# Reordering TensorE between the threshold verdict and the first output projections, and a projection that waits for a residual instead of a variance

## The chip, the cores and the metric

The kernel runs on one core of one Trainium2 chip. The metric is the device time of one execution in microseconds (us). A core has five engines that run instruction streams of their own and meet at semaphores: TensorE (PE; its weight loads are PEld), VectorE (DVE), ScalarE (ACT), GpSimd (POOL) and SyncE (SP), which issues most of the DMAs.

## The reference, cut to what matters

Sixteen sequences of 128 rows with 256 features, x, pass through four gated layers, each added to x. The two in the middle matter here.

```python
# layer 2: a sparse feed-forward net, on h = layernorm(x), 2048 rows
z = h @ ternary_quant(W_syn).T + b_syn            # 2048 x 1024
thresh = top_k(z, 102)[0][:, -1:]                 # a threshold for every row
hidden = where(z >= thresh, relu(z), 0.0)
out = hidden @ ternary_quant(W_out).T + b_out     # the output projection
x = x + tanh(g_ffn[0]) * (layernorm(h + out) * gamma + beta)

# layer 3: a long convolution; k = v = ctx, q = layernorm(x)
kv = einsum('bhil,bhjl->bijhl', k_, v_)
y = irfft(rfft(kv) * rfft(ssm_kernel)) + kv * D   # does not depend on x
x = x + tanh(g_xattn[1]) * einsum('bijhl,bhil->bjhl', y, q_)
```

Layer 1 is an attention over features, layer 4 a mixture of 64 experts with six chosen for every row.

## The kernel before, in words

The rows are worked on in 16 tiles (b = 0 to 15) of 128 rows. The kernel has stages: attention and z for all tiles; the search for the 16 x 128 thresholds; the batch pipeline (projection, second norm, layer 3's last product, routing), in which tiles go in pairs through a loop v_ = 0 to 7 (NPAIR = 8) that every engine's program writes out in an order of its own; then the experts, and the sum of their outputs. No planner orders anything: each engine executes its list in order, and semaphore waits stand in it.

**The convolution of layer 3** needs no x. It is made head by head, 16 of them, k = 0 to 15: `conv(k)` (TensorE, L932) does six products of 344 columns on the products of k and v (`kv_in`, by DMA), a Toeplitz matrix, and a diagonal (`tdiag_ready`). `keep_conv(k)` (ScalarE, L1311) copies four PSUM banks out and counts `co_ready`. SyncE stores the copy to `co_rows` in HBM (L513, `co_out`). AHEAD = 14 of them, k = 0 to 13, stand beside the threshold search, in two sets of PSUM banks in turn: 0 to 3 for even k, 4 to 7 for odd k. Numbers 14 and 15 use banks 4 to 7 and stand among the first projections. When all sixteen stores have landed, SyncE loads `co_rows` back by pairs of tiles, `load_group(g)` (L517, the DMA at L520), and then issues 36 fills of `xs_rows` (L443) before group 2.

**The verdict.** VectorE finds a threshold for each row in a few steps and tells whether any row failed: `verdict` (L1823) makes `bad` and counts `bad_ready`. TensorE sums `bad` over partitions with one narrow matmul into the first column of bank 0 (L960). VectorE copies the sum as an integer (L1849), makes the hidden tiles 0 and 1 by the thresholds (L1846, counting `hid_made`), loads the integer, skips the repair branch when it is zero, and counts `hid_ready` by two (L1886).

**A tile's projection.** `turn_hidden(b)` (TensorE, L962) transposes hidden tile b with eight transposes into banks 1 and 2; it waits until tile b-1 was copied out. `evac_hidden(b)` (ScalarE, L1351) copies it to SBUF. `project(b)` (TensorE, L972) is 16 matmuls of 256 columns into bank 0. VectorE's `second_block(b)` (L1922) makes hidden tile b+2, then adds the projection to the residual `H2` (`residual`, L1895), takes row sums, aggregates, and writes mean and variance (L1920, counting `var3_ready`); between these stand the four steps of tile b-1, which end in `x` after layer 2 and its own variance. GpSimd raises the variances to -0.5.

**Then layer 3's last product**: `query3` (ScalarE, L1358), `turn_q` (TensorE), `evac_q` (ScalarE), and `times_q(h)` (VectorE, L1946; its first instruction is L1959), which waits for the group of `co_rows` that was loaded back (`kv_in`) and for its query. The first, `times_q(0)`, stands on VectorE behind `second_block(2)`; `second_block(3)` stands behind it. A pair's scatters to the experts' rows (`scatters`, GpSimd, L781) wait for the routing of that pair, and the first pair's also for all the fills.

The orders around the change, before:

```python
# TensorE
for k in range(AHEAD): conv(k)
pe.wait_ge(co_ready, AHEAD); pe.wait_ge(bad_ready, 1)      # L958, L959
pe.matmul(psum[:, 0, 0:1], onesf, bad).then_inc(ones_done)  # L960
conv(AHEAD); turn_hidden(0); turn_hidden(1); project(0); conv(AHEAD + 1)
# then, for v_ = 0: turn_hidden(2), project(1), turn_hidden(3), project(2)
# ScalarE
keep_conv(AHEAD); evac_hidden(0); evac_hidden(1); keep_conv(AHEAD + 1)
# then, for v_ = 0: evac_hidden(2), evac_hidden(3)
```

Of the kernel before, what the change touches and what calls it, by code (L numbers as in the profile page):

```python
# [18 lines left out]
def build(nc, x, ctxn, ctxT, ctxH, toep, gates_in, wsynT, woutT, bsyn, bout, gamma, beta, ssm_D,  # L19
          gateT, wexp, wd1, wsgu, wsd, out):  # L20
    f32, bf16, i32, u32 = mybir.dt.float32, mybir.dt.bfloat16, mybir.dt.int32, mybir.dt.uint32
    ALU = mybir.AluOpType
# [4 lines left out]
    NT = 16  # L27
    D = 256
# [34 lines left out]
    AHEAD = 14  # L63
# [21 lines left out]
    with ExitStack() as ctx:  # L85
# [12 lines left out]
        H2 = sb("H2", [P, NT, D])  # L98
# [29 lines left out]
        stats = sb("stats", [P, NT + 2, 6])  # L128
# [10 lines left out]
        wsc = sb("wsc", [P, 2])  # L139
# [119 lines left out]
        psum = ctx.enter_context(nc.psum_tensor("psum", [P, 8, 512], f32))  # L259
# [25 lines left out]
        var3_ready, rstd3_ready = sem("var3_ready"), sem("rstd3_ready")  # L285
# [25 lines left out]
        hid_made = sem("hid_made")  # L311
# [12 lines left out]
        conv_done, co_ready = sem("conv_done"), sem("co_ready")  # L324
# [70 lines left out]
        def alone(eng, name):  # L395

            eng.sem_inc(tick[name], 1)
# [469 lines left out]
        def _(pe):  # L867
# [64 lines left out]
            def conv(k):  # L932
                w = 8 * NCOL
                first = 4 * (k % 2) if k < AHEAD else 4
                pe.wait_ge(tdiag_ready, 2 * k + 2)
                if k < DIRECT:
                    src = kv_sq[:, head_of(k) % 2].rearrange("p m b r -> p (m b r)")
                    pe.wait_ge(kv_ready, head_of(k) + 1)
                else:
                    src = kvs[k % 4]  # L940
                    pe.wait_ge(kv_in[k % 4], 16 * ((k - DIRECT) // 4) + 16)
                if k >= 2:
                    pe.wait_ge(co_ready, k - 1 if k < AHEAD else k)
                for g in range(2):
                    r = [src[:, (16 * m_ + 8 * g) * NCOL:(16 * m_ + 8 * g + 8) * NCOL] for m_ in range(2)]
                    pe.matmul(psum[:, first + g, 0:w], tdiags[k % 4], r[0], start=True, stop=True)  # L946
                    pe.matmul(psum[:, first + 2 + g, 0:w], toeps[k % 4][:, 1, :], r[0], start=True, stop=False)  # L947
                    m = pe.matmul(psum[:, first + 2 + g, 0:w], tdiags[k % 4], r[1], start=False, stop=True)  # L948
                m.then_inc(conv_done, 1)
# [3 lines left out]
            pe.wait_ge(hT_ready, NT)  # L953
            pe.wait_ge(w_ready, 2)
            pe.wait_ge(z_ready, NT)
            for k in range(AHEAD):
                conv(k)
            pe.wait_ge(co_ready, AHEAD)  # L958
            pe.wait_ge(bad_ready, 1)  # L959
            pe.matmul(psum[:, 0, 0:1], onesf[:, :], bad[:, :], start=True, stop=True).then_inc(ones_done, 1)  # L960

            def turn_hidden(b):  # L962
                par = b % 2
# [8 lines left out]
            def project(b):  # L972
                par = b % 2
                pe.wait_ge(hidT_ready, b + 1)
                if b:
                    pe.wait_ge(var3_ready, b)
                for c in range(8):
                    m = pe.matmul(psum[:, 0, 0:D], hidT[:, par, c * P:(c + 1) * P], wout[:, c, :],  # L978
                                  start=(c == 0), stop=(c == 7))
                m.then_inc(o_done, 1)  # L980
# [78 lines left out]
                                      wsd_sb[0:fw, c, :], start=(c == 0), stop=(c == 2))  # L1059
                m.then_inc(sy_done, 1)  # L1060

            conv(AHEAD)
            turn_hidden(0)
            turn_hidden(1)
            project(0)
            conv(AHEAD + 1)
            for v_ in range(NPAIR):
                c, u, w = v_ - 1, v_ - 2, v_ - 3
                if u >= 0:
                    x3_turn(u)  # L1070
                if c >= 0:
                    turn_q(2 * c)
                if 2 * v_ + 2 < NT:
                    turn_hidden(2 * v_ + 2)
                project(2 * v_ + 1)
                if w >= 0:
                    shared_up(w, 2)
                if c >= 0:
                    turn_q(2 * c + 1)
                if w >= 0:  # L1080
                    shared_down(w)
                if u >= 0:
                    if u == 0:
                        pe.wait_ge(co_ready, NH)
                        pe.wait_ge(ws_in, 64)
                    r_turns(u)
                if 2 * v_ + 3 < NT:
                    turn_hidden(2 * v_ + 3)
                if u >= 0:
                    logits(u)  # L1090
                if 2 * v_ + 2 < NT:
                    project(2 * v_ + 2)
                if 0 <= u < NPAIR - 3:
                    ranks(u)
                    shared_up(u, 0)
                    shared_up(u, 1)

            a, b = NPAIR - 2, NPAIR - 1
# [142 lines left out]
        def _(act):  # L1241
# [69 lines left out]
            def keep_conv(k):  # L1311
                par = k % 2
                first = 4 * par if k < AHEAD else 4
                act.wait_ge(conv_done, k + 1)
                if co_turn[k]:
                    act.wait_ge(co_out[co_slot[k]], 16 * co_turn[k])
                for l in range(2):
                    m = act.activation(co[co_slot[k]].rearrange("p (g a l n) -> p l g a n", g=2, a=4, l=2)[:, l],
                                       psum[:, first + 2 * l:first + 2 * l + 2, 0:8 * NCOL].rearrange("p g (a n) -> p g a n", a=4),
                                       ACT.Copy)  # L1320
                m.then_inc(co_ready, 1)
# [29 lines left out]
            def evac_hidden(b):  # L1351
                act.wait_ge(hidT_full, b + 1)
                if b >= 2:
                    act.wait_ge(o_done, b - 1)
                act.activation(hidT[:, b % 2, :].rearrange("p (a n) -> p a n", a=2), psum[:, 1:3, :],  # L1355
                               ACT.Copy).then_inc(hidT_ready, 1)
# [55 lines left out]
                act.wait_ge(sy_done, w + 1)  # L1412
                act.activation(base[:, w], s_y[:, :], ACT.Identity, scale=tg[:, 3:4]).then_inc(base_ready, 1)

            keep_conv(AHEAD)
            evac_hidden(0)
            evac_hidden(1)
            keep_conv(AHEAD + 1)
            for v_ in range(NPAIR):
                c, u, w = v_ - 1, v_ - 2, v_ - 3  # L1420
                if c >= 0:
                    query3(2 * c)
                if u >= 0:
                    keep_rows(u)
                if c >= 0:
                    evac_q(2 * c)
                if 2 * v_ + 2 < NT:
                    evac_hidden(2 * v_ + 2)
                if w >= 0:
                    shared_silu(w, 2)  # L1430
                if c >= 0:
                    query3(2 * c + 1)
                    evac_q(2 * c + 1)
                if u >= 0:
                    normalise(u)
                if w >= 0:
                    shared_out(w)
                if u >= 0:
                    evac_x(u)
                if 2 * v_ + 3 < NT:  # L1440
                    evac_hidden(2 * v_ + 3)
                if 0 <= u < NPAIR - 3:
                    keep_logits(u)
                    exponents(u)
                    shared_silu(u, 0)
                    shared_silu(u, 1)
# [66 lines left out]
        def _(dve):  # L1513
            v = {"at": 0, "k": 0}

            def mark(ins):

                v["k"] += 1
                ins.then_inc(v_step, 1)
                return v["at"] + v["k"]  # L1520
# [374 lines left out]
            def residual(b, par):  # L1895
                dve.wait_ge(o_done, b + 1)
                dve.wait_ge(h2b_done, b + 1)
                return mark(dve.scalar_tensor_tensor(H2[:, b, :], psum[:, 0, 0:D], wsc[:, 1:2], H2[:, b, :], ALU.mult, ALU.add))

            def centre(b):  # L1900
                dve.wait_ge(rstd3_ready, b + 1)
# [6 lines left out]
            def row_sums(src, slot_, made):  # L1908
                dve.wait_ge(v_step, made)
                alone(dve, "dve")  # L1910
                return mark(dve.bn_stats(stats[:, slot_, :], src))
# [10 lines left out]
            def second_block(b, between=None):  # L1922
                tile, behind = b < NT, b >= 1
                if b + 2 < NT:
                    make_hidden(b + 2, b % 2)
                if tile:
                    at_h = residual(b, b % 2)
                if behind:
                    at_x = centre(b - 1)
                if between is not None:  # L1930
                    mean_shift(between)
                if tile:
                    at_h = row_sums(H2[:, b, :], NT, at_h)
                if behind:
                    at_x = add2(b - 1, at_x)
                if tile:
                    at_h = aggregate(NT, at_h)
                if behind:
                    at_x = row_sums(X[:, b - 1, :], NT + 1, at_x)
                if tile:  # L1940
                    variance(b, NT, at_h, var3_ready)
                if behind:
                    at_x = aggregate(NT + 1, at_x)
                    variance(b - 1, NT + 1, at_x, var4_ready)
# [332 lines left out]
```

## Time and profile before

| what | value |
|---|---|
| median of three runs | 716.46 us (712.61 to 722.75) |
| the profiled execution | 720.17 us, of which its span is 718.4 us |
| mean granted TensorE clock of the span | 0.944 of full speed |
| TensorE matmul busy | 611.0 us (85% of the span) |
| VectorE busy | 471.6 us (66%) |
| GpSimd busy | 451.8 us (63%) |
| ScalarE busy | 296.9 us (41%) |

The span runs from the first to the last instruction of the profiled execution; times in the trace count from its start. Busy times are sums over stages with different limits, so a stage is read from its own stretch. The threshold search ends near 180 us, the batch pipeline lies between 180 and 415 us, the experts' matmuls between 423 and 651 us.

### The profile page before, as it was taken

How to read it: one execution, taken by the hardware profiler on the slowest of the kernel's cores; microseconds unless marked ns; L12 is line 12 of the kernel's file. 1: busy time of each engine (PE TensorE's matmuls, PEld its weight loads, DVE VectorE, ACT ScalarE, POOL GpSimd, SP SyncE). 2: the span in 40 equal slices, each digit the busy share in tenths (PEclk: the TensorE clock that was granted, in tenths of full speed). 3: DMA queues.
4: the chain of work that ended last, by engine and by line, in shares of the span. 5: the costliest groups of instructions: out<-in, count | busy, mean ns of one | idle time of the engine just before them, and what ended most of it. 6: DMA issues, size and time to landing. Idle time of an engine off the chain costs nothing.

```text
span 718.4 us, 11813 instructions
## 1 busy us (share of the span) xinstructions
PE 611.0 (85%) x3072; PEld 470.5 (65%) x3072; DVE 471.6 (66%) x1596; ACT 296.9 (41%) x657; POOL 451.8 (63%) x512
## 2 busy tenths in 40 slices
PE   4789998769788798989857879999999999999920
PEld 2455554446566677877746668888888888878710
DVE  5898987999259988898895534444454454544515
ACT  3157777958233454555455223322233232323200
POOL 2697845782022287878787724777777777786560
PEclk9799999989899999999989899999999999999965
DMA  7579715869959943953333768999999999996878
GB/s 243 181 255 317 258 46 186 231 181 304 317 195 376 373 160 130 309 203 115 150 109 129 237 217 209 240 284 256 281 249 284 258 263 278 264 271 105 231 122 295
DMA packets 97822, 163.69 MB, mean 228 GB/s; under 512 B 10848, under 2 KB 65568, under 8 KB 96736
## 3 DMA queue, kind: packets, MB, share of 16 engines
q1 hardware_dynamic: 76864, 135.16, 56.9%
q0 software_dynamic: 20608, 27.82, 20.2%
q8 instruction: 23, 0.38, 0.2%
q14 instruction: 39, 0.32, 0.1%
q10 hardware_dynamic: 288, 0.01, 0.0%
HBM read 91.24 MB, written 71.71 MB: 227 GB/s over the span
## 4 chain that ended last, share of the span: by engine, by line
PE 57%; DVE 14%; issue 11%; POOL 9%; DMA 6%; ACT 1%; SPq 1%; DVEq 0%; POOLq 0%; ACTq 0%
PE psum L1164 12%; PE psum L1177 7%; PE psum L1168 6%; PE psum L904 5%; POOL xs_rows L781 5%; PE psum L1182 4%; PE psum L1148 4%; PE psum L1048 3%; PE psum L978 3%; PE psum L946 3%; PE psum L947 3%; PE psum L948 2%; DMA acc<-hh,toki 2%; POOL acc L847 2%; DVE Z L1962 1%
## 5 line engine op out<-in xcount | busy, mean ns | idle before, releaser
L847 POOL DMA_INDIRECT acc<-hh,toki x128 | 187.9, 1468 | 80.4 <-DVE hh L2173 40.9
L2173 DVE TENSOR_SCALAR hh<-psum,wtok 96x256 f32<-96x256 f32 (+3 forms) x128 | 55.8, 478 | 131.8 <-issue 110.7
L781 POOL DMA_INDIRECT xs_rows<-Z,slot x96 | 101.6, 1058 | 33.5 <-issue 23.4
L1481 ACT ACTIVATE qT<-psum 128x384 f32<-128x384 f32 (+3 forms) x64 | 33.5, 524 | 91.9 <-PE psum L1148 91.0
L694 POOL TENSOR_TENSOR rstd<-mv,neghalf 128x1 f32<-128x1 f32 x48 | 32.4, 685 | 59.9 <-DVE mv L1920 41.5
L978 PE MATMUL psum<-wt,hh 128*128 128x256 f32 x256 | 59.2, 385 | 4.5 <-DVE mv L1920 3.4
L904 PE MATMUL psum<-wt,hTs 128*128 128x512 f32 x128 | 59.7, 609 | 0.6 <-ACT hTs L1260 0.6
L978 PEld LDWEIGHTS psum<-wt,hh 128*128 128x128 f32 x256 | 48.0, 192 | 11.3 <-ACT hh L1355 4.6
L1164 PE MATMUL psum<-qT,kve 128*128 128x192 f32 (+3 forms) x256 | 52.8, 350 | 0.0
L1048 PE MATMUL psum<-Z,wt 128*128 128x256 f32 (+1 forms) x192 | 48.7, 406 | 0.8 <-DVE H L2035 0.8
L1487 ACT ACTIVATE H<-psum 128x192 f32<-128x192 f32 (+3 forms) x64 | 22.2, 348 | 63.7 <-PE psum L1164 62.0
L1164 PEld LDWEIGHTS psum<-qT,kve 128*128 128x128 f32 x256 | 43.6, 194 | 1.5
L1164 PE MATMUL psum<-qT,Z 128*128 128x192 f32 (+3 forms) x224 | 44.2, 340 | 0.0
L1048 PEld LDWEIGHTS psum<-Z,wt 128*128 128x128 f32 (+1 forms) x192 | 36.4, 194 | 7.8 <-DVE H L2035 1.0
L904 PEld LDWEIGHTS psum<-wt,hTs 128*128 128x128 f32 x128 | 23.5, 194 | 24.0 <-issue 24.0
L1148 PE MATMUL psum<-ident,Z 96*128 96x96 f32 (+3 forms) x256 | 35.9, 263 | 2.2 <-DMA Z<-xs_rows 2.2
L1164 PEld LDWEIGHTS psum<-qT,Z 128*128 128x128 f32 x224 | 37.0, 190 | 0.6
L1148 PEld LDWEIGHTS psum<-ident,Z 96*128 96x128 f32 (+3 forms) x256 | 27.4, 142 | 15.0 <-issue 12.2
L1274 ACT ACTIVATE hh<-Z,thr 128x1024 bf16<-128x1024 f32 x32 | 36.7, 1146 | 1.2 <-DVE Z L1655 0.6
L1182 PE MATMUL psum<-wt,hh 48*96 48x256 f32 (+3 forms) x240 | 33.4, 397 | 0.0
L1489 ACT ACTIVATE H<-psum 48x192 f32<-48x192 f32 (+3 forms) x64 | 21.8, 341 | 23.5 <-PE psum L1168 23.5
L876 PE MATMUL psum<-hh,kve 128*128 128x256 f32 x64 | 20.3, 447 | 12.2 <-DVE hh L1601 7.7
(368 smaller groups left out, 1434.9 us busy)
## 6 DMA issues: line engine op xcount, KB each, us to landing
xs_rows<-fill SPq DMA_DIRECT2D x64, 272.0 KB, 4.5
kve<-in_wexp SPq DMA_DIRECT2D x32, 496.0 KB, 4.1
Z<-in_wexp SPq DMA_DIRECT2D x30, 496.0 KB, 4.3
kve<-co_rows SPq DMA_DIRECT2D x8, 1376.0 KB, 7.5
kv_rows<-Z SPq DMA_DIRECT2D x8, 688.0 KB, 3.9
kve<-kv_rows SPq DMA_DIRECT2D x8, 688.0 KB, 7.9
Z<-xs_rows SPq DMA_DIRECT2D x24, 204.0 KB, 4.2
Z<-xs_rows SPq DMA_DIRECT2D x16, 272.0 KB, 3.1
```

What stands on the lines that cost most here:

```text
L781: pool.indirect_dma_start(out=xs_rows[:, :], out_offset=bass.IndirectOffsetOnAxis(ap=slot[:, t, k:k + 1], axis=0), in_=H[:, t, :], in_offs ...
L847: pool.indirect_dma_start(out=acc[a][:, :], out_offset=bass.IndirectOffsetOnAxis(ap=toki[0:p, g, j:j + 1], axis=0), in_=y_sb[0:p, s, j, :] ...
L904: m = pe.matmul(psum[:, 4 + 2 * par + c, :], hTs[:, par, k, :], wsyn[:, k, c * 512:(c + 1) * 512], start=(k == 0), stop=(k == 1))
L978: m = pe.matmul(psum[:, 0, 0:D], hidT[:, par, c * P:(c + 1) * P], wout[:, c, :], start=(c == 0), stop=(c == 7))
L1048: m = pe.matmul(s_up[w][c][0:fw, g * CAP:(g + 1) * CAP], wsgu_sb[:, k, g * FSH + f0:g * FSH + f0 + fw], xTs[:, w, k, :], start=(k == 0), s ...
L1148: m = pe.transpose(pT[par][:, (2 * k + j) * p:(2 * k + j + 1) * p], xs_sb[0:p, s, j, k * P:(k + 1) * P], ident[0:p, 0:p])
L1164: m = pe.matmul(pA[par][:, g * CAP:g * CAP + 2 * p], w[:, k, g * P:(g + 1) * P], xT[:, par, k, 0:2 * p], start=(k == 0), stop=(k == 1))
L1168: m = pe.matmul(pC[par][0:GU - 2 * P, 0:2 * p], w[:, k, 2 * P:GU], xT[:, par, k, 0:2 * p], start=(k == 0), stop=(k == 1))
L1177: pe.matmul(pY[q][0:p, j * D:(j + 1) * D], hid0[:, q, j * p:(j + 1) * p], lastd0[:, s - 4 + q, :] if last else wd0_sb[s + q], start=(j == ...
L1182: m = pe.matmul(pY[q][0:p, j * D:(j + 1) * D], hid1[r, q, j * p:(j + 1) * p], lastd1[r, (s - 4) // 2, :] if last else wd1_sb[r, s + q, :], ...
L1274: act.activation(ajunk[:, i % 4, :], z[:, t, :], ACT.Sign, bias=points[:, t:t + 1], scale=-1.0, accum_out=total[:, t:t + 1]).then_inc(cnt_ ...
L2173: m = dve.tensor_scalar(y_sb[0:p, s, j, :], pY[par][0:p, j * D:(j + 1) * D], wtok[0:p, g, j:j + 1], None, ALU.mult)
```

## The change

On TensorE the verdict's sum is put between the convolutions of heads 12 and 13, and waits for 13 copies, not 14. Head 13 follows it. Heads 14 and 15 each move one place back: 14 from before the first transposes to behind `project(0)`, 15 from behind `project(0)` to behind `project(1)`. ScalarE's copies of 14 and 15 move to match. Besides, `project(b)` no longer waits for the variance of tile b-1 (`var3_ready`) but for the residual that reads bank 0 (`hid_made`, now counted on by `residual`), and the row sums of the residual wait on that same count.

```diff
@@ TensorE
-            for k in range(AHEAD):
+            for k in range(AHEAD - 1):
                 conv(k)
-            pe.wait_ge(co_ready, AHEAD)
+            pe.wait_ge(co_ready, AHEAD - 1)
             pe.wait_ge(bad_ready, 1)
             pe.matmul(psum[:, 0, 0:1], onesf[:, :], bad[:, :], start=True, stop=True).then_inc(ones_done, 1)
+            conv(AHEAD - 1)
...
             def project(b):
                 pe.wait_ge(hidT_ready, b + 1)
                 if b:
-                    pe.wait_ge(var3_ready, b)
+                    pe.wait_ge(hid_made, b + 2)
...
-            conv(AHEAD)
             turn_hidden(0)
             turn_hidden(1)
             project(0)
-            conv(AHEAD + 1)
+            conv(AHEAD)
...
                 project(2 * v_ + 1)
+                if v_ == 0:
+                    conv(AHEAD + 1)
@@ ScalarE
-            keep_conv(AHEAD)
             evac_hidden(0)
             evac_hidden(1)
-            keep_conv(AHEAD + 1)
+            keep_conv(AHEAD)
...
                 if 2 * v_ + 2 < NT:
                     evac_hidden(2 * v_ + 2)
+                if v_ == 0:
+                    keep_conv(AHEAD + 1)
@@ VectorE
             def residual(b, par):
-                return mark(dve.scalar_tensor_tensor(H2[:, b, :], psum[:, 0, 0:D], wsc[:, 1:2], H2[:, b, :], ALU.mult, ALU.add))
+                dve.scalar_tensor_tensor(H2[:, b, :], psum[:, 0, 0:D], wsc[:, 1:2], H2[:, b, :], ALU.mult, ALU.add).then_inc(hid_made, 1)
...
                 if tile:
-                    at_h = residual(b, b % 2)
+                    residual(b, b % 2)
...
                 if tile:
-                    at_h = row_sums(H2[:, b, :], NT, at_h)
+                    dve.wait_ge(hid_made, b + 3)
+                    alone(dve, "dve")
+                    at_h = mark(dve.bn_stats(stats[:, NT, :], H2[:, b, :]))
```

## Rows read from the trace of the kernel before

**Rows 1.** The page's busy time, share of the span and instructions.

```profile
PE 611.0 (85%) x3072; PEld 470.5 (65%) x3072; DVE 471.6 (66%) x1596; ACT 296.9 (41%) x657; POOL 451.8 (63%) x512
```

**Rows 2.** The chain that ended last, 181 to 246: start us, us, what.

```profile
181.26 1.39 ACT co L1318 x2
...
182.69 0.38 PE psum L960 x2
183.07 1.68 issue
184.75 1.49 PE psum L946 x2
...
191.24 1.38 ACT qT L1318 x2
...
208.41 3.71 PE psum L978 x16
...
214.76 0.43 DVE Z L1959
...
217.70 1.11 issue
...
245.68 0.24 DVE mask L2005
```

**Rows 3.** The timeline from 177 to 186, VectorE and ScalarE.

```profile
177.79 1.38 ACT L1318 ACTIVATE wt<-psum 128x688 f32<-128x688 f32 x2 [0.65 <-PE psum L948]
...
178.11 0.15 DVE L1828 TENSOR_SCALAR bad<-bad 128x1 f32<-128x1 f32 x1
...
183.18 0.16 DVE L1849 CAST bad_i<-psum 128x1 int32<-128x1 f32 x1 [3.81 <-PE psum L960]
183.25 2.47 DVE L1846 SCALAR_TENSOR_TENSOR hh<-Z,thr 128x1024 f32<-128x1024 f32 x2
```

**Rows 4.** The timeline from 194 to 208, TensorE, ScalarE and SyncE.

```profile
194.57 3.62 PE L978 MATMUL psum<-wt,hh 128*128 128x256 f32 x16
...
198.03 0.74 PE L946 MATMUL psum<-kve,hs 128*128 128x344 f32 x2
...
201.50 1.04 PE L968 MATMUL psum<-ident,hh 128*128 128x128 f32 x8
201.70 1.38 ACT L1318 ACTIVATE qT<-psum 128x688 f32<-128x688 f32 x2 [5.90 <-PE psum L948]
...
202.37 3.62 PE L978 MATMUL psum<-wt,hh 128*128 128x256 f32 x16
...
203.11 0.36 SPq L513 DMA_DIRECT2D co_rows<-qT  x1
...
207.34 0.81 SPq L520 DMA_DIRECT2D kve<-co_rows  x2
```

**Rows 5.** DMA issues at 174.1, 203.1, 207.3 and 241.5 to 242.5: us to landing.

```profile
kve<-kv_rows SPq DMA_DIRECT2D x1, 688.0 KB, 10.5
...
co_rows<-qT SPq DMA_DIRECT2D x1, 688.0 KB, 4.2
...
kve<-co_rows SPq DMA_DIRECT2D x1, 1376.0 KB, 5.7
...
xs_rows<-fill SPq DMA_DIRECT2D x2, 272.0 KB, 3.9
```

**Rows 6.** By stretch: length, busy PE, PEld, DVE, ACT, POOL, PE clock, DMA, GB/s.

```profile
181.00:184.70 3.70, 0.60 (x3) 0.30 (x2) 1.52 (x3) 1.38 (x2) 1.02 (x2) 0.83 1.13 296
184.70:190.20 5.50, 5.45 (x10) 3.36 (x11) 1.02 (x1) 0.00 (x0) 0.45 (x1) 0.50 1.06 374
190.20:195.00 4.80, 3.20 (x22) 2.60 (x21) 1.28 (x1) 2.52 (x4) 0.00 (x0) 0.99 1.18 282
```

**Rows 7.** TensorE's waits from 205 to 235: us in total, times, longest us.

```profile
PE psum L978 <- DVE mv L1920: 3.4, 3, 1.5
```

**Rows 8.** The timeline at the first scatter, GpSimd.

```profile
248.47 2.00 POOL L781 DMA_INDIRECT xs_rows<-Z,slot  x1 [7.02 <-DVE slot L2028]
```

## The prediction

> **What bounds the kernel now.** I read the page's busy shares first, and only to see that they decide nothing: TensorE has 85% and VectorE 66% of the span [rows 1], averages over stages. The question is what holds up the stretch that the change touches, so I went on to the chain that ended last between 181 and 246 us [rows 2]. The reader should see three parts in it. First the verdict: the chain goes through ScalarE's copy of head 13 (181.26), the narrow sum (182.69), a pause of 1.68 us, and head 14 on TensorE from 184.75. Then the projections, with head 15 between them, up to the third one at 208.41. Then it passes to VectorE: the first `times_q` begins at 214.76 and the chain stays on VectorE to the routing mask at 245.68. So for the end it counts when that first `times_q` starts, not when a projection does.
>
> Then the timeline around the verdict [rows 3]: `bad` is made at 178.11 + 0.15 = 178.26, but its integer is read at 183.18 only. In between TensorE finished head 13 and ScalarE copied it, because the sum waits for 14 copies. Last the rows of the other thing that `times_q(0)` needs, the convolutions loaded back [rows 4, 5]: the store of head 15 is issued at 203.11 and takes 4.2 us to land; the load of group 0 goes out at 207.34, and lands 5.7 us later, at 213.04. That is only 214.76 - 213.04 = 1.72 us before `times_q(0)` began. This second chain runs through head 15, which the change moves behind one more projection.
>
> **The change part by part.** The pitches come from rows 4. Head 15's first matmul comes at 198.03 and the transposes behind it at 201.50: a head costs 3.47 us of TensorE. From its first matmul to its copy's start: 201.70 - 198.03 = 3.67. To the issue of its store: 203.11 - 198.03 = 5.08. Transposes to projection: 202.37 - 201.50 = 0.87. A projection to what follows it: 198.03 - 194.57 = 3.46. From a copy of a head to the first projection, with two transposed tiles and ScalarE's copies between: 194.57 - 191.24 = 3.33 [rows 2, 4].
>
> (1) The sum. It now waits for `bad` (178.26) and the copy of head 12, which ends at 177.79 + 1.38 = 179.17 [rows 3]; before it began 0.05 after the copy, so at 179.2 instead of 182.69, 3.5 us earlier. Queued behind it on TensorE is head 13, which before ran without a pause; this adds an idle TensorE from head 12's end (177.8) to 179.2, and head 13 begins behind the sum's 0.38, at 179.59. VectorE's tiles 0 and 1 move with the sum: from 183.25 + 2.47 = 185.72 to 182.2. The thresholds still count one branch after that; before, head 14 covered it, now head 13 does, which ends near 183.2.
>
> (2) Heads 13 to 15 and the first projections. Copy of 13 starts at 179.59 + 3.67 = 183.26. `project(0)` starts 3.33 later, 186.59, against 194.57: 8.0 earlier. Of these, 2.8 are the half clock of head 14 (184.75 to its copy at 191.24 is 6.49, against 3.67), 1.7 the pause in front of it, the rest the sum's place. That pause I read as the load of head 14's products, issued at 174.1 with 10.5 to land, so 184.6 [rows 5]. In the new order head 14 starts at 186.59 + 3.46 = 190.05, and the load is hidden with 5.4 us to spare. Transposes of tile 2 at 193.52, `project(1)` at 194.39, head 15 at 197.85. Before it was 198.03. So the 8.0 us are spent on what now stands in front of head 15 besides, a head, a tile's transposes and a projection, 3.47 + 0.87 + 3.46 = 7.8, and head 15 moves by -0.2.
>
> (3) After head 15: transposes at 201.32, `project(2)` at 202.19 against 208.41, 6.2 earlier. VectorE would reach `times_q(0)` at 214.76 - 6.2 = 208.5.
>
> (4) What is late next. The store of head 15 goes out at 197.85 + 5.08 = 202.93, group 0 is issued 0.18 earlier than before and lands at 212.86. `times_q(0)` starts there, near 212.9, not at 208.5. SyncE's queue holds nothing else against it: the stores of 12 to 14 are issued earlier or land before 207. The gain at the handover is 214.76 - 212.9 = 1.86, rounded 1.8; the other 4.4 us are idle time of VectorE. Bounds: nothing at all, if the load lands 1.7 later, and 6.3, if it does not bind.
>
> (5) The projection's wait for the variance. TensorE waited for it three times, 3.4 us in all and at most 1.5 [rows 7], and all three lie between 205 and 235 us. The first is already in step (3), where `project(2)` is held by the transposes alone. The other two lie where the chain is on VectorE, so they pay nothing at the end; without them TensorE idles elsewhere. Cost below: none, since the new count rises at an earlier instruction of the same block. On VectorE the row sums wait for the same instruction as before by another semaphore; no instruction is added.
>
> (6) Downstream. Through 245.68 VectorE's list is the chain; it moves by 1.8. The first scatter at 248.47 waited for a slot [rows 8] and would be due at 246.7; the last fills, issued by 242.5 with 3.9 to land, are in by 246.4 [rows 5]. That is close, but holds. After it everything follows the same orders, so I carry 1.8 to the end: 718.4 for the profiled execution (720.17). That one lies 3.7 above the median of the runs shown; measured times are medians, so I forecast 716.46 - 1.8 = 714.7 us.
>
> **The rivals.** (A) The clock falls, and head 15 comes late: slower. In 181.00 to 184.70 TensorE was busy 0.60 us, and the next 5.5 us were granted 0.50, the lower level of 1.2 GHz [rows 6]. The new order has a pause of 1.4 us before the sum, and between head 13 and `project(0)` 3.3 us with nothing but 16 transposes. At the lower level a head takes 6.49 instead of 3.67, 1.77 times as long; a projection would take 6.1 instead of 3.46, the transposes nearly 1 more, so head 15 comes about 3.4 later, group 0 at 216.3, and `times_q(0)` 1.5 late: 718.0 us. It decides from the point where head 15 is more than 1.9 later than I put it. Against it: in 190.20 to 195.00 the same transposes, with the same pause for ScalarE between them, were granted 0.99 [rows 6]. For it: the pause before the sum comes on top.
>
> The Trainium skill, in "TensorE: Matmul & The Clock Gate", section "Part 4: PE-mode transpose", says that transposes do not count as activity for the full clock as matmuls do. By that rule the stretch before `project(0)` looks idle to the chip and rival A is what happens, 718.0 instead of 714.7. The row of 190.20 to 195.00, with 0.99, speaks against it here.
>
> (B) The gain is given back: 716.5. VectorE's new wait before `times_q(0)` leaves TensorE without work between `project(3)` and tile 5's transposes, some 6 us, after which it could run at the lower level until the first pair's transposes of layer 3 are late by 1 to 2 us; or the last fills hold the first scatter. That would also be the case in which the edits do what they say, and none of it is on the path.
>
> (C) Group 0 does not bind, and all of step (3) stays: 716.46 - 6.3 = 710.2. It needs head 15's store and reload to end by 208.5, and the rows give them 4.2 and 5.7 from 202.9 on; and the fills would then stop the first scatter after some 2 us.
>
> **How the numbers follow.** Forecast 0.60, A 0.17, B 0.18, C 0.05. All four lie between 710.2 and 718.0. The runs before spread from 3.9 below to 6.3 above their median, which is more than the cases differ, so the range is 708.5 to 720.5: the cases with about 2 us of spread at each end. Two per cent is 14.3 us, about what a measurement of this kernel can tell from no change, and no case reaches it. Only an error in which the whole trace is misread would: faster 0.03, within 0.95, slower 0.02.
>
> **What would show it.** Right: the integer of `bad` is read near 179.7 and the first hidden tiles are ready by 182.3; `project(0)` near 186.6 and `project(2)` near 202.2; VectorE idle for some 4 us before L1959, which starts within 0.2 us of group 0's landing near 212.9; no wait of L978 on L1920; the first scatter near 246.7. Wrong: a granted clock of 0.5 between 180 and 195, head 15 after 199, or an L1959 that starts well before 212, or a first scatter that has not moved though L1959 has.

## The result, and the profile after

The change makes no difference of two per cent, but it is slower, not faster as forecast. Its median is 722.29 us over 20 runs, that of the kernel before 718.48 over 20 runs that include the three shown; the ratio is 1.0071, 95% interval 1.0048 to 1.0095, some 5.1 us. (The ratio is an estimate over the runs and not the quotient of the two medians, which differ by 3.8 us.) The forecast was 1.8 us less, 714.7, and the measured median lies above the upper end of the range, 720.5. Of the 7.6 us between 714.7 and 722.29, 2.0 are the base that the forecast started from: the three runs shown had a median of 716.46, the twenty have 718.48. The profiled execution took 720.8 us with a mean granted clock of 0.942, much like that of before. On the page nothing moves that could tell why:

```profile
PE 610.8 (85%) x3072; PEld 472.8 (66%) x3072; DVE 470.7 (65%) x1596; ACT 296.3 (41%) x657; POOL 451.3 (63%) x512
```

Against [rows 1] the busy times differ by 1 us or less, except for the weight loads, which overlap. So the stretch has to be read. The timeline of the changed kernel, 181 to 251 us (start, us, engine, line; in brackets the idle time in front and what ended it):

```profile
181.07 0.15 DVE L1831 TENSOR_SCALAR bad<-bad 128x1 f32<-128x1 f32 x1
...
181.37 0.35 PE L960 MATMUL psum<-bad,onesf 128*128 128x1 f32 x2 [3.65 <-DVE bad L1831]
...
181.58 1.03 PE L946 MATMUL psum<-kve,tdiag 128*128 128x344 f32 x2
...
187.03 1.38 ACT L1320 ACTIVATE co<-psum 128x688 f32<-128x688 f32 x2 [7.89 <-PE psum L948]
...
205.97 3.62 PE L979 MATMUL psum<-wt,hh 128*128 128x256 f32 x16
...
216.82 0.43 DVE L1964 TENSOR_TENSOR Z<-kve,hTs 128x256 f32<-128x256 f32 x1 [4.51 <-DMA kve<-co_rows]
...
250.53 2.00 POOL L781 DMA_INDIRECT xs_rows<-Z,slot  x1 [7.02 <-DVE slot L2033]
```

The reader should see four things. The verdict came at 181.07, not at 178.11 [rows 3] (two executions, of which more below), and since head 13 now stands behind the sum, TensorE waited 3.65 us for it. The third projection (205.97) did come earlier, by 2.4 us against 208.41 [rows 2]. The store of head 15 (206.70, in the next view) came 3.6 later than 203.11 [rows 4]. And the first `times_q` stood idle for 4.51 us until the load of group 0 had landed, and began at 216.82 instead of 214.76, 2.06 late; the first scatter at 250.53 is 2.06 behind [rows 8]. The chain of waits says the same; where [rows 2] had the third projection it now has two transfers (start us, us, what):

```profile
206.70 4.27 DMA co_rows<-qT
...
211.04 5.75 DMA kve<-co_rows
```

TensorE's waits between 205 and 235 us hold no wait of a projection on the variance any more, against three in [rows 7]; the one large wait left is that of tile 5's transposes on VectorE:

```profile
PE psum L969 <- DVE hh L1849: 7.4, 1, 7.4
```

It ends at 222.19, and behind it the grant fell to 0.50 in the last of the windows below. The first scatter did not feel it: it stands 33.71 us behind the first `times_q` here, as it did before (248.47 - 214.76).

The windows of the changed kernel, with busy times by engine and, behind them, the granted TensorE clock as a share of full speed:

```profile
177.70:181.40 3.70, 0.05 (x2) 0.06 (x1) 3.49 (x11) 1.38 (x2) 0.00 (x0) 1.00 1.09 326
181.60:185.50 3.90, 3.90 (x10) 2.39 (x10) 3.21 (x6) 0.00 (x0) 1.03 (x2) 0.56 1.14 296
185.50:190.00 4.50, 2.90 (x18) 2.15 (x18) 1.28 (x1) 2.29 (x3) 0.46 (x1) 1.00 1.07 378
...
220.00:225.00 5.00, 2.81 (x11) 2.63 (x12) 4.82 (x12) 0.80 (x1) 0.53 (x2) 0.50 0.99 338
```

After the idle 3.70 us head 13 ran near the lower level, 0.56. In the stretch of the 16 transposes that rival A feared (185.50 to 190.00) the grant was 1.00.

### The profile page after: what moved, and what is told of

Its sections match the earlier page's. It is cut to its first block, busy times and chain, and to the rows that moved or that the text cites. A ratio compares the mean times of both kernels' runs of the same rounds, so it can differ in the third digit from the quotient of the medians.

```text
span 719.0 us, 11813 instructions
## 1 busy us (share of the span) xinstructions
PE 610.8 (85%) x3072; PEld 472.8 (66%) x3072; DVE 470.7 (65%) x1596; ACT 296.3 (41%) x657; POOL 451.3 (63%) x512
## 4 chain that ended last, share of the span: by engine, by line
PE 52%; DVE 17%; issue 12%; DMA 8%; POOL 7%; ACT 3%; SPq 0%; DVEq 0%; POOLq 0%; ACTq 0%
PE psum L1166 12%; PE psum L1179 7%; PE psum L1170 6%; PE psum L904 5%; POOL xs_rows L781 5%; PE psum L1184 4%; PE psum L1150 4%; PE psum L1049 3%; PE psum L979 3%; DVE hh L1815 3%; DMA acc<-hh,toki 2%; POOL acc L847 2%; PE psum L876 2%; DVE Z L1966 1%; DVE Z L1967 1%
```

## The experiments

Four theories were put to the chip. H: the end follows the store of head 15, through its reload, and the change puts more in front of that store. S: the sum's place does it, by the pause and the half clock behind it. W: the new wait for the residual does it. P: the projections decide. A fifth, L, came up on the way and stands with its run. Ratios are against the kernel before, run beside it, each over 12 runs of the kernel, with the 95% interval. Where a head moves on TensorE, ScalarE's copy of it moves to match (in the sixth experiment its order already fits); those lines are left out of the diffs.

**Only the new wait** (before, with the second half of the change; VectorE's lines, as in the change, are left out):

```diff
-                    pe.wait_ge(var3_ready, b)
+                    pe.wait_ge(hid_made, b + 2)
```

> The kernel before with one part of the change: a projection waits for the last tile's residual instead of its variance; TensorE's and ScalarE's orders stay. Theory H (the change is slower because head 15's store, and with it the reload of group 0, comes later): no difference, ratio 0.998 to 1.002, the store of head 15 near 203 us. Theory S (the sum of the verdict in front of head 13 makes TensorE pause and then run at half clock, that alone costs the time): no difference either. Theory W (the new wait does the harm, by letting projections run where they disturb VectorE or the transposes): slower, ratio near 1.007.

Measured: 719.13 us, ratio 1.0008 (0.9976 to 1.0040). W falls. The timeline of this kernel showed something unforeseen; the store was expected near 203:

```profile
182.41 0.38 PE L960 MATMUL psum<-bad,onesf 128*128 128x1 f32 x2 [1.47 <-ACT co L1318]
...
198.28 0.36 SPq L513 DMA_DIRECT2D co_rows<-qT  x1
...
208.51 0.46 DVE L1961 TENSOR_TENSOR Z<-kve,hTs 128x256 f32<-128x256 f32 x1 [0.24 <-DMA kve<-co_rows]
```

The sum (182.41) is close to where it was in [rows 2] (182.69), and the order from there to head 15 is that of before; yet the store is out 15.87 us behind the sum, not 20.42.

**Only the order** (the change, with the old wait back):

```diff
-                    pe.wait_ge(hid_made, b + 2)
+                    pe.wait_ge(var3_ready, b)
```

> The changed kernel with the variance wait put back in the projection: the order alone. H and S: as slow as the whole change, ratio 1.005 to 1.009, store of head 15 near 206 to 207 us. W: no slower than before, ratio 1.000.

Measured: 722.92 us, ratio 1.0060 (1.0028 to 1.0092). The order alone is as slow as the whole change. Its timeline, and its windows before and in head 13:

```profile
181.57 0.35 PE L960 MATMUL psum<-bad,onesf 128*128 128x1 f32 x2 [3.08 <-DVE bad L1831]
...
205.21 0.36 SPq L513 DMA_DIRECT2D co_rows<-qT  x1
...
215.66 0.43 DVE L1964 TENSOR_TENSOR Z<-kve,hTs 128x256 f32<-128x256 f32 x1 [4.83 <-DMA kve<-co_rows]
```

```profile
178.40:181.50 3.10, 0.10 (x1) 0.00 (x0) 2.89 (x11) 1.38 (x2) 0.00 (x0) 1.00 1.07 358
181.60:185.50 3.90, 3.90 (x15) 2.46 (x16) 3.55 (x7) 0.00 (x0) 1.03 (x2) 1.00 1.14 310
```

Head 13 was granted 1.00 here, and still the store is 23.64 us behind the sum. No clock is needed for the loss.

**The sum back behind head 13**, the heads 14 and 15 where the change has them:

```diff
-            for k in range(AHEAD - 1):
+            for k in range(AHEAD):
                 conv(k)
             pe.wait_ge(co_ready, AHEAD - 1)
...
-            conv(AHEAD - 1)
```

> The changed kernel with the sum of the verdict put back behind head 13 (it still waits for 13 copies only); heads 14 and 15 stay one place back. S: the loss is gone, ratio 0.998 to 1.002, because TensorE no longer pauses in front of head 13. H: a loss remains, ratio 1.002 to 1.008: by the rows of before the sum at 181.3, first projection at 187.4, head 15 at 198.7 and its store at 203.7, against 203.1, and 2 to 3 us later than that if the clock falls in the pause before the transposes.

Measured: 724.05 us, ratio 1.0080 (1.0047 to 1.0114). The pause in front of the sum is gone and the loss is not. A pause and a half clock came behind the sum instead, so this run alone does not clear the clock; the run before it, with the loss at full clock, does. Together they let S fall. Timeline and windows:

```profile
182.81 0.28 PE L960 MATMUL psum<-bad,onesf 128*128 128x1 f32 x2
...
208.57 0.36 SPq L513 DMA_DIRECT2D co_rows<-qT  x1
...
218.63 0.43 DVE L1963 TENSOR_TENSOR Z<-kve,hTs 128x256 f32<-128x256 f32 x1 [4.44 <-DMA kve<-co_rows]
```

```profile
183.20:187.30 4.10, 1.05 (x8) 0.86 (x8) 2.86 (x5) 1.19 (x2) 0.75 (x2) 1.00 1.14 300
187.40:194.20 6.80, 5.66 (x18) 4.88 (x19) 1.26 (x1) 2.02 (x2) 0.45 (x1) 0.50 1.09 341
```

With no head behind the sum TensorE was busy 1.05 us of 4.10, and the next 6.80 us were granted 0.50. This is the fall that rival A described, in a neighbour of the change. Idle time and transposes stand together in that stretch, so it cannot be told which of them brought it.

**The heads back, the sum early** (the change, with 14 and 15 in their old places):

```diff
+            conv(AHEAD)
             turn_hidden(0)
             turn_hidden(1)
             project(0)
-            conv(AHEAD)
+            conv(AHEAD + 1)
...
-                if v_ == 0:
-                    conv(AHEAD + 1)
```

> The changed kernel with heads 14 and 15 back in their old places (14 in front of the first transposes, 15 behind the first projection); the sum stays in front of head 13. S: as slow as the change, ratio 1.005 to 1.009. H: not slower than before, ratio 0.995 to 1.001, head 15's store issued at 200.2 to 202.5 us, the first product of layer 3 on VectorE 0.6 to 2.9 us earlier than the 214.76 of before.

Measured: 719.84 us, ratio 1.0009 (0.9981 to 1.0038). The loss goes with the heads' places, so H holds. In the profiled execution the store was later than the 200.2 to 202.5 that H expected, and `times_q(0)` no earlier than in [rows 2], but 0.28 later; timeline, and the window of head 13:

```profile
182.05 0.35 PE L960 MATMUL psum<-bad,onesf 128*128 128x1 f32 x2 [3.30 <-DVE bad L1829]
...
204.85 0.36 SPq L513 DMA_DIRECT2D co_rows<-qT  x1
...
215.04 0.43 DVE L1962 TENSOR_TENSOR Z<-kve,hTs 128x256 f32<-128x256 f32 x1 [0.21 <-DMA kve<-co_rows]
```

```profile
182.20:187.40 5.20, 5.20 (x14) 3.12 (x14) 3.42 (x6) 0.00 (x0) 1.13 (x2) 0.67 1.10 329
```

The verdict was late again, TensorE waited 3.30 us for it, and head 13 was granted 0.67. The early sum had bought a pause.

**Only head 15 moved back** (before, nothing else):

```diff
             project(0)
-            conv(AHEAD + 1)
...
                 project(2 * v_ + 1)
+                if v_ == 0:
+                    conv(AHEAD + 1)
```

> The kernel before with one edit: head 15 behind the second projection instead of the first (TensorE and ScalarE). Theory H (the end follows the store of head 15 by its reload): one tile's transposes and a projection more in front of it, 0.87 + 3.46 = 4.3 us, so its store 4.3 us after where the same execution would have had it, near 202.6 to 207.4, and slower by 2.6 to 4.3 us (the smaller where the reload has slack), ratio 1.0035 to 1.006. A rival, theory P (the end follows the projections; head 15 does not matter): no slower, since the projections come 3.5 us earlier, ratio at most 1.000.

Measured: 722.53 us, ratio 1.0059 (1.0030 to 1.0087).

```profile
184.92 0.38 PE L960 MATMUL psum<-bad,onesf 128*128 128x1 f32 x2 [1.47 <-DMA kve<-kv_rows]
...
206.27 0.36 SPq L513 DMA_DIRECT2D co_rows<-qT  x1
...
216.69 0.43 DVE L1961 TENSOR_TENSOR Z<-kve,hTs 128x256 f32<-128x256 f32 x1 [4.80 <-DMA kve<-co_rows]
```

One move costs what the whole change costs. `times_q(0)` is 31.77 us behind the sum and was idle for 4.80 in front of it: the projections were ready, so P falls and H holds.

**Head 15 in front of the first projection** (before, the other way):

```diff
             turn_hidden(1)
+            conv(AHEAD + 1)
             project(0)
-            conv(AHEAD + 1)
```

> The kernel before with one edit: head 15 in front of the first projection, behind the two tiles' transposes. H: its store 3.5 us earlier, near 194.8 to 199.6; the reload then does not bind, the first product of layer 3 follows the third projection instead, which keeps its place, so a gain of 0 to 1.7 us, ratio 0.997 to 1.000. P: slower by up to 3.5 us for the first projection's later start, ratio up to 1.005.

Measured: 718.43 us, ratio 1.0009 (0.9978 to 1.0040).

```profile
180.72 0.38 PE L960 MATMUL psum<-bad,onesf 128*128 128x1 f32 x2 [1.47 <-ACT co L1318]
...
193.14 0.36 SPq L513 DMA_DIRECT2D co_rows<-qT  x1
...
209.39 0.43 DVE L1959 TENSOR_TENSOR Z<-kve,hTs 128x256 f32<-128x256 f32 x1
```

The store is out 12.42 us behind the sum, group 0 lands at 205.02, and `times_q(0)` does not wait for it: it stands 6.34 us behind the third projection (203.05). The reload now has 4.4 us to spare, and that buys nothing, since the projections are next; the third stands 22.33 us behind the sum, against 21.17 in the second profile of before, below.

**Four fills moved** from SyncE's loop over the heads to the first stage. The loop also issues the heads' loads; two of the four fills stand in front of head 14's load, two behind it. Theory L: the pause and the half clock behind the sum, 4.5 us, come from that load being behind the fills.

```diff
-                    if DIRECT // 2 <= k < AHEAD - 2:
+                    if DIRECT // 2 <= k < DIRECT:
...
+                if 10 <= b < 14:
+                    fill_rows(b + 16, b + 17)
```

> The kernel before with four fills of xs_rows (heads 8 to 11 of SyncE's store loop) moved into the first stage. Theory L (in some executions of before head 14 waits for its products' load, issued behind fills, and runs at half clock after the pause): the load of head 14 issued near 171 and landed before 182, no pause between the verdict's sum and head 14, head 15's store near 198 as in the execution of the first experiment, time 1 to 5 us shorter, ratio 0.993 to 0.999. If the loads behind fills do not matter: 1.000.

Measured: 717.64 us, ratio 1.0002 (0.9972 to 1.0033). A miss for L: the pause is gone from its profile, and by the ratio the time has not followed (the medians differ by 1.8 us, 717.64 against 719.46).

```profile
182.49 0.38 PE L962 MATMUL psum<-bad,onesf 128*128 128x1 f32 x2 [1.47 <-ACT co L1320]
...
182.73 0.82 PE L948 MATMUL psum<-kve,hs 128*128 128x344 f32 x2
...
198.36 0.36 SPq L515 DMA_DIRECT2D co_rows<-qT  x1
...
210.01 0.42 DVE L1961 TENSOR_TENSOR Z<-kve,hTs 128x256 f32<-128x256 f32 x1
```

Head 14 follows the sum in 0.24 us, and the store comes 15.87 us behind the sum, to the hundredth as in the run of the wait alone, where the fills stood in their place. That raised the question whether before's pause was ever typical.

**Before and the change, profiled once more.**

> The kernel before once more, for a second profile of it. H and L: if its span is some 4 us shorter than the first profile's 718.4, the store of head 15 lies near 198 to 199 and no half clock follows the verdict's sum; if it is as long, the store lies near 203. The verdict is expected near 180.5 to 182.4, as in the five other profiles, not at 178.3.

> The changed kernel once more, for a second profile. H: the first product of layer 3 starts within 0.1 us of group 0's landing, its store of head 15 23.6 to 25.3 us behind the verdict's sum, against 15.9 in the kernel before where nothing pauses; the sum waits for the verdict, which is 2 to 4 us behind the end of head 12.

Measured: 719.11 and 723.35 us, one run each. The second profile of before, timeline and the window of head 14 and the transposes:

```profile
184.96 0.38 PE L960 MATMUL psum<-bad,onesf 128*128 128x1 f32 x2 [1.47 <-ACT co L1318]
...
185.20 0.82 PE L946 MATMUL psum<-kve,hs 128*128 128x344 f32 x2
...
200.83 0.36 SPq L513 DMA_DIRECT2D co_rows<-qT  x1
...
206.13 3.69 PE L978 MATMUL psum<-wt,hh 128*128 128x256 f32 x16 [1.54 <-DVE mv L1920]
...
212.48 0.43 DVE L1959 TENSOR_TENSOR Z<-kve,hTs 128x256 f32<-128x256 f32 x1
```

```profile
185.20:192.00 6.80, 5.20 (x28) 3.75 (x28) 3.83 (x4) 2.29 (x3) 0.46 (x1) 1.00 1.09 348
```

No pause, clock 1.00, and again 15.87 from the sum to the store and 27.52 to `times_q(0)`, where the first profile had 20.42 and 32.07 [rows 2 to 4]. Neither case of the expectation came: the span, 717.4, is only 1.0 shorter than the first, and yet there is no half clock, and the store is at 200.83. Of the 4.55 us saved behind the sum, 2.27 were lost in front of it (184.96 against 182.69) and 1.2 behind `times_q(0)`. So one execution's time does not tell whether it had the pause. The second profile of the change:

```profile
182.00 0.38 PE L960 MATMUL psum<-bad,onesf 128*128 128x1 f32 x2 [1.47 <-ACT wt L1320]
...
205.67 0.36 SPq L513 DMA_DIRECT2D co_rows<-qT  x1
...
215.96 0.43 DVE L1964 TENSOR_TENSOR Z<-kve,hTs 128x256 f32<-128x256 f32 x1 [4.67 <-DMA kve<-co_rows]
```

```profile
182.00:190.00 8.00, 6.40 (x34) 4.87 (x35) 4.03 (x4) 2.75 (x4) 2.11 (x3) 1.00 1.09 345
190.00:200.00 10.00, 10.00 (x48) 8.09 (x47) 2.45 (x5) 2.86 (x4) 1.88 (x2) 1.00 0.99 276
```

Here the sum waits 1.47 us for ScalarE's copy, as the prediction had it and not for the verdict, as had been expected by then, and the clock is 1.00 throughout. The store is 23.67 us behind the sum, and 23.67 - 15.87 = 7.8, the very figure of step (2).

**The change with head 15 directly behind head 14**, in front of tile 2's transposes and `project(1)`:

```diff
             conv(AHEAD)
+            conv(AHEAD + 1)
...
-                if v_ == 0:
-                    conv(AHEAD + 1)
```

> The changed kernel with head 15 directly behind head 14, in front of tile 2's transposes and the second projection; all else as changed. Theory H: the store of head 15 comes 4.3 us earlier for the work that it passes, less some 1.6 us in which it waits for the copy of head 14 out of the same banks, so 2.7 us earlier than in the changed kernel (22.3 us or less behind the verdict's sum, instead of 23.6 to 25.3), and about half of the loss is gone, ratio to before 1.002 to 1.005. If the place of head 15 did not matter: 1.006 to 1.008 as the change.

Measured: 720.08 us, ratio 1.0016 (0.9991 to 1.0040); the value lies a little under the 1.002 to 1.005 that H expected, the interval overlaps that range and holds 1 as well, and it leaves out the 1.006 to 1.008 of a place that does not matter. In the profile the store is 21.13 us behind the sum, and the reload still comes last:

```profile
180.23 0.38 PE L960 MATMUL psum<-bad,onesf 128*128 128x1 f32 x2 [1.47 <-ACT wt L1319]
...
201.36 0.36 SPq L513 DMA_DIRECT2D co_rows<-qT  x1
...
211.59 0.46 DVE L1962 TENSOR_TENSOR Z<-kve,hTs 128x256 f32<-128x256 f32 x1 [0.24 <-DMA kve<-co_rows]
```

**What the experiments point to**: before's order, head 15 in front of `project(0)`, the new wait, and the four fills moved (the edits of the first, the sixth and the seventh experiment together).

> A try at a version faster than both: the kernel before with the projection waiting for the residual (first experiment), head 15 in front of the first projection, and four fills moved into the first stage. H: the reload has slack (store of head 15 some 12.4 us behind the sum), the third projection starts 19.3 us behind the sum instead of 21.2, and the first product of layer 3 follows it by 6.3: 25.7 us behind the sum instead of 27.5 in the kernel before, a gain of about 1.8 us, ratio 0.996 to 1.000. If neither the reload nor the third projection decides: 1.000.

Measured: 716.75 us, ratio 0.9966 (0.9934 to 0.9997), some 2.4 us faster than before, with an interval that only just leaves out 1; against before, the change has 1.0071, so it is faster than the change, too.

```profile
187.51 0.38 PE L962 MATMUL psum<-bad,onesf 128*128 128x1 f32 x2 [1.47 <-ACT co L1320]
...
213.40 0.43 DVE L1963 TENSOR_TENSOR Z<-kve,hTs 128x256 f32<-128x256 f32 x1
```

`times_q(0)` is 25.89 us behind the sum, 1.6 less than in the second profile of before, and it follows the third projection again (207.00), which now starts right behind its transposes, without the 1.54 us for the variance.

**All profiles side by side.** In each of the 13 the last instruction ends 498.1 to 501.8 us behind the start of `times_q(0)`, with no order between the kernels (498.1 and 501.6 in the two profiles of the change), so what an edit changes is when that starts. The spread of 3.7 us is close to the size of the effects, though: a single profile shows the mechanism and not the time. Where the reload comes last it starts 0.02 to 0.03 us behind group 0's landing; elsewhere 6.3 to 6.4 us behind the third projection. From the store to the landing are 9.9 to 10.4 us (11.9 in the sixth experiment, whose store alone took 6.2). All columns are us; "sum ahead of old place" is how much earlier the sum is than 8.57 us behind the first matmul of head 12, where before's order has it (182.69 - 174.12). The last column but one is the distance to `times_q(0)` less 27.52, less the column before it.

| kernel | sum to store of 15 | sum to `times_q(0)` | comes last | sum ahead of old place | so against before | measured |
|---|---|---|---|---|---|---|
| before, first profile | 20.42 | 32.07 | projection | 0 | +4.6 | |
| before, second | 15.87 | 27.52 | projection | -0.1 | +0.1 | |
| change, first profile | 25.33 | 35.45 | reload | 1.3 | +6.6 | +5.1 (3.4 to 6.8) |
| change, second | 23.67 | 33.96 | reload | 3.5 | +3.0 | the same |
| order only | 23.64 | 34.09 | reload | 1.8 | +4.8 | +4.3 (2.0 to 6.6) |
| sum behind 13 | 25.76 | 35.82 | reload | 1.3 | +7.0 | +5.7 (3.4 to 8.2) |
| heads in place | 22.80 | 32.99 | reload | 1.6 | +3.9 | +0.6 (-1.4 to 2.7) |
| 15 behind 14 | 21.13 | 31.36 | reload | 3.5 | +0.4 | +1.1 (-0.6 to 2.9) |
| 15 back | 21.35 | 31.77 | reload | -0.6 | +4.9 | +4.2 (2.2 to 6.3) |
| wait only | 15.87 | 26.10 | reload | -0.1 | -1.3 | +0.6 (-1.7 to 2.9) |
| 15 first | 12.42 | 28.67 | projection | 0 | +1.2 | +0.6 (-1.6 to 2.9) |
| fills early | 15.87 | 27.52 | projection | 0 | 0 | +0.1 (-2.0 to 2.4) |
| all together | 12.41 | 25.89 | projection | 0 | -1.6 | -2.4 (-4.7 to -0.2) |

The measured column is the ratio less one, times 718.48. By the difference of the medians each entry would be 0.2 to 1.9 us lower. Of the profiles beside a measured value all but two lie inside its interval. The second of the change is just under it (3.0 against 3.4). "Heads in place" lies above it, 3.9 against at most 2.7. The low clock of its head 13 does not explain that: the execution profiled took 719.73 us, and the median of its twelve runs is 719.84. Why these runs lose less than the profile's distances say is open. The wait alone has the other sign, inside its interval.

## Why the prediction was wrong

- **Step (1), the sum 3.5 us earlier: overestimated.** It was measured at 3.5 in one profile of the change, and at 1.3 in the other. The step put the verdict where [rows 3] had it, 4.1 us behind the first matmul of head 12. Over the 13 profiles it comes 3.2 to 7.1 us behind that (181.22 - 174.09 = 7.1 in the change). In before's order head 13 covers this, since the sum stands behind it anyway; in the change TensorE stands idle for it, 3.65 us at most, and may run head 13 at a lower granted clock: its first matmul to its copy was 5.45 us, not 3.67. Why VectorE's verdict moves so much from one execution to another was not found.
- **Step (2), head 15 moved by -0.2: this is the step that failed.** It spent a gain of 8.0 us (3.5 sum, 2.8 half clock, 1.7 pause) on 7.8 of extra work. The 7.8 is right: 23.67 - 15.87. So is the distance that follows from the step: 202.93 - 179.2 = 23.7 from the sum to the store, 23.67 in the second profile of the change. What was wrong is what it was compared with. But the 2.8 and the 1.7 belonged to the one profiled execution of before; its second profile, the wait alone and the moved fills have neither, and the stores there stand 15.87 behind the sum. Five profiles have head 14 right behind the sum and its load behind the same fills (before twice, the wait alone, head 15 moved back, head 15 first); in four of them it starts 0.24 to 0.25 us behind the sum. So a gain of 4.5 us was booked that four of these five do not have to give, and up to 2.2 too much for the sum. That the one profile at hand had the pause was bad luck; that it was taken for the kernel's own was the step's error. Where the store of before comes 15.87 behind the sum, the change makes it later by 7.8 less the 1.3 to 3.5 of the sum, 4.3 to 6.5 us, and `times_q(0)` by that less the reload's 1.66 us of slack (below), 2.6 to 4.8, before any low clock.
- **Step (3): right behind the sum.** It put the third projection at 202.19 - 179.2 = 23.0 behind the sum; in the second profile of the change it is 22.94. In that of before it is 21.17 (206.13 - 184.96), with a head less in between and a wait of 1.54 for the variance, so that here too the 6.2 us of gain were mostly the first profile's own pause and clock.
- **Step (4), the reload binds: right**, within 0.03 us in both profiles, and VectorE is idle for 4.51 and 4.67 us, where "some 4" was forecast. What was wrong is the time at which it lands: in an execution without before's pause the reload has 1.66 us to spare (212.48 - 210.82), and the change takes that and more.
- **Step (5), the wait pays nothing beyond step (3): right** for the change (the order alone measures the same), and by the wait alone (1.0008). It is worth something only where the reload has slack: the third projection stands 19.47 us behind the sum with the wait alone (201.88 - 182.41) against 21.17, and the last experiment, where the projections come last, keeps 1.6 of it.
- **Step (6), carried to the end: right as far as the first scatter**, with the wrong sign carried: it moved by the same 2.06 us as `times_q(0)`. From there to the end two executions differ by more than that: the spans of these two profiles are 718.4 and 719.0.
- **Rival A** had the sign and the place, head 15 late past the reload's slack, but not the cause: the second profile and the order alone have full clock between sum and store, and the store is 7.8 later behind it. In the two profiles of the change the clock adds 1.8 us at most, in head 13, behind the pause for the verdict. Of rival **B** the mechanism came, and not the price: TensorE stood idle for 7.43 us in front of tile 5's transposes, the next 5 us were granted 0.50 (220.00 to 225.00), and the first scatter is no further behind `times_q(0)` for it. There was no gain to give back. Rival **C** did not happen.
- **The base**: 2.0 of the 7.6 us of the miss are the median of three runs, 716.46, that the forecast was subtracted from. That is luck and not mechanism; with the median of twenty the forecast would have been 716.7, with the same wrong sign.

The Trainium skill, in "TensorE: Matmul & The Clock Gate", section "Part 4: PE-mode transpose", says that transposes do not count as work for the full clock the way matmuls do. The change's own rows, 1.00 from 185.50 to 190.00, do not bear out a fall there; the 0.50 with the sum behind 13 does not decide it, since 3.15 us of idle time stand in front of the transposes.

## What to carry to other kernels

Before a gain is booked from a pause or a low clock that a profile shows, look whether it belongs to the kernel or to that one execution: a second profile of the kernel before would have changed the sign here. Where two chains meet within 2 us, count what each move puts in front of either; the work put in front of head 15 was exact to 0.1 us, and with the first profile's pause left out it gives the sign. An early consumer of another engine's result should keep some independent work in front of it to absorb that engine's spread; this is drawn from the waits of 3.08 to 3.65 us for the verdict in three profiles, and no run tests it by itself.

## What the runs showed of the hardware

- The same instructions in the same order took 15.87 us from the sum to the store of head 15 in three profiles, to the hundredth, and 20.42 in a fourth. In that one TensorE stood still for 1.68 us behind the sum, and the next 5.5 us were granted 0.50 [rows 6].
- An idle stretch did not always cost the clock: behind 3.10 us with 0.10 busy (order only) the grant was 1.00; behind 3.70 us with 0.05 busy (the change) it was 0.56. Behind the 7.43 us without work in the change it was 0.50.
- The store of head 15 and the reload behind it took 9.9 to 10.4 us in sequence in twelve profiles, though the orders on TensorE differ, and 11.9 in one; the two transfers were 4.27 and 5.75 us in the change, near the 4.2 and 5.7 of [rows 5].
